# First experts of a four-block tower: up products by windows of 16 images, three of them without the class rows, and a ring for the split hidden rows

## The reference, cut to what matters

```python
h = conv tokens + position table                     # 25 patches an image
h = concat([broadcast(cls_tok), h], axis=1)          # the class token comes first
h = h + L0_attn(layernorm(h))                        # causal: token t sees tokens 0..t
x = layernorm(h)
g = softmax(x @ gate_w + gate_b)                     # 32 gates a token
for e in range(32):
    hid = gelu(x @ w1[e] + b1[e])                    # 192 -> 768
    h  += g[..., e] * (hid @ w2[e] + b2[e])          # 768 -> 192
```

## Time and profile before

| | us |
|---|---|
| median of 3 runs | 3105.53 (3105.32 to 3115.47) |
| the profiled execution | 3103.02, its span 3101.2 |
| TensorE busy | 2909.5, mean granted clock 0.961 |
| VectorE busy | 2093.5 |
| ScalarE busy | 1067.5 |
| GpSimd busy | 616.4 |

### The profile page before, as it was taken

One profiled execution on the slowest core, in us unless ns is written; L12 is line 12 of the kernel. 1 busy time (PEld: TensorE's weight loads), 2 busy tenths in 40 slices (PEclk: granted clock), 3 DMA queues, 4 the chain that ended last, 5 costly groups with the idle time before them and its releaser, 6 DMA issues. The chain is left out here.

```text
span 3101.2 us, 56587 instructions
## 1 busy us (share of the span) xinstructions
PE 2909.5 (94%) x20015; PEld 2670.3 (86%) x20015; DVE 2093.5 (68%) x5315; ACT 1067.5 (34%) x2124; POOL 616.4 (20%) x807
## 2 busy tenths in 40 slices
PE   9899999999999999999998998897998899958888
PEld 7779999999999999999997888675777889957677
DVE  3857677767767777777776776333448667777876
ACT  2533333323333333333233333112435433324433
POOL 1312111221212121111212100112213201122450
PEclk9989999999999999999999999798999989989999
DMA  3001100000100000000000000372000100000000
GB/s 136 26 30 36 37 18 36 36 36 18 36 36 19 35 36 36 18 36 36 18 31 9 2 2 2 94 240 73 1 11 1 54 19 19 1 11 16 23 19 17
DMA packets 24461, 105.56 MB, mean 34 GB/s; under 512 B 4455, under 2 KB 9463, under 8 KB 19086
## 3 DMA queue, kind: packets, MB, share of 16 engines
q1 hardware_dynamic: 22654, 99.62, 9.2%
q0 software_dynamic: 1584, 3.30, 0.3%
HBM read 98.32 MB, written 6.64 MB: 34 GB/s over the span
## 5 line engine op out<-in xcount | busy, mean ns | idle before, releaser
L907 ACT ACTIVATE hid<-bank,dat 128x384 f32<-128x384 f32 (+1 forms) x912 | 555.5, 610 | 1144.3 <-PE bank L597 1031.7
L872 PE MATMUL bank<-w,hid_hi 128*128 128x384 f32 x2964 | 859.3, 361 | 2.2 <-DVE y_tok L923 1.6
L874 PE MATMUL bank<-w,hid_lo 128*128 128x192 f32 x2964 | 745.8, 252 | 0.0
L874 PEld LDWEIGHTS bank<-w,hid_lo 128*128 128x128 f32 x2964 | 571.3, 193 | 1.7
L872 PEld LDWEIGHTS bank<-w,hid_hi 128*128 128x128 f32 x2964 | 561.7, 190 | 5.5 <-issue 3.9
L941 DVE TENSOR_TENSOR hid_lo<-hid,hid_hi 128x384 fp32r<-128x384 f32 (+1 forms) x912 | 540.0, 592 | 31.5
L938 DVE CAST hid_hi<-hid 128x384 fp32r<-128x384 f32 (+1 forms) x912 | 340.9, 374 | 126.4 <-ACT hid L907 125.3
L964 DVE SCALAR_TENSOR_TENSOR h_tok<-bank,gate,h_tok 128x192 f32<-128x192 f32 x416 | 173.5, 417 | 247.2 <-PE bank L874 243.8
L597 PE MATMUL bank<-xa_hi,w_hi 128*128 128x384 f32 (+1 forms) x912 | 324.6, 356 | 7.6 <-DVE w_lo L750 4.7
L597 PE MATMUL bank<-xa_lo,w_hi 128*128 128x384 f32 (+1 forms) x912 | 323.1, 354 | 0.0
L597 PE MATMUL bank<-xb,w_lo 128*128 128x384 f32 (+1 forms) x912 | 322.7, 354 | 0.0
(11 more groups left out here) (361 smaller groups left out, 4383.0 us busy)
## 6 DMA issues: line engine op xcount, KB each, us to landing
raw<-in_L_exp SPq DMA_DIRECT2D x36, 1344.0 KB, 5.6
w_e<-in_L_exp SPq DMA_DIRECT2D x20, 576.0 KB, 4.0
w_e<-in_L_exp SPq DMA_DIRECT2D x20, 384.0 KB
pix<-in_pixels SPq DMA_DIRECT2D x6, 832.0 KB, 10.2
w_e<-in_L_exp SPq DMA_DIRECT2D x20, 195.0 KB
raw<-in_L_mlp SPq DMA_DIRECT2D x2, 1344.0 KB, 5.7
wp_raw<-in_L_att SPq DMA_DIRECT2D x1, 2304.0 KB, 8.3
route_rows<-in_rows_clear SPq DMA_DIRECT2D x1, 2000.0 KB, 23.1
```

Of the source, the lines that this page charges most:

```text
L872: nc.tensor.matmul(o[:, 0:2 * D], hid_hi[k % 2][:, m, c], w2[j][:, m, :], start=m == 0, stop=False)
L874: ins = nc.tensor.matmul(o[:, 0:D], hid_lo[k % 2][:, m, c], w2[j][:, m, 0:D], start=False, stop=m == HC - 1)
L907: nc.scalar.activation(hid[(6 * k + m) % 3][:, 0:128 * nt], bank[4 + (6 * k + m) % 4][:, 0:128 * nt], func, bias=bias).then_inc(s["h_act"] ...
```

## The change

All experts now work by windows of 16 images, 416 columns, instead of 384 or 512. With `one_class=True`, which only the 32 first experts get, windows 1, 2 and 3 leave out the class column of each image in the up products and in the activation: the moving operand becomes a view of 25 slots by 16 images, image innermost, so that neighbouring columns lie 26 elements apart. The results stand side by side in the bank (400 columns), and ScalarE writes them back to their places in `hid`, with the same step. `hid` becomes six buffers of 416 columns, one for each m; its class columns are written in window 0 of each expert, and windows 1 to 3 leave them as they are. All 416 columns are still split, and the down products still run by the same 13 tiles.

`hid_hi` and `hid_lo` become one ring each of 896 columns (seven tiles). Since windows and tiles have different lengths, tile t is read at `RING_OF_TILE[t]`, and window 2 is written in two pieces, at the end and at the start of the ring.

```diff
+WINDOW = 16 * SLOT
+RING = 896
+RING_OF_WINDOW = [[(0, 416, 0)], [(0, 416, 416)], [(0, 64, 832), (64, 416, 0)], [(0, 416, 352)]]
+RING_OF_TILE = [0, 128, 256, 384, 512, 640, 768, 0, 128, 256, 384, 512, 640]
...
-        hid_hi = [sb("hid_hi0", [128, HC, 512], F32R, ex)]
+        hid = [sb(f"hid{j}", [128, WINDOW], scope=ex) for j in range(HC)]
...
-        hid = [sb(f"hid{j}", [128, 512], scope=ex) for j in range(3)]
-        hid_hi.append(sb("hid_hi1", [128, HC, 512], F32R, ex))
-        hid_lo = [sb(f"hid_lo{j}", [128, HC, 512], F32R, ex) for j in range(2)]
+        hid_hi = sb("hid_hi", [128, HC, RING], F32R, ex)
+        hid_lo = sb("hid_lo", [128, HC, RING], F32R, ex)
...
+            def patches(x, k):
+                return x.rearrange("p (m s) -> p s m", s=SLOT)[:, 1:, :] if one_class and k else x
+            def width(k):
+                return WINDOW - WINDOW // SLOT if one_class and k else WINDOW
+            def product_of(o, k):
+                o = o[:, 0:width(k)]
+                return o.rearrange("p (s m) -> p s m", m=WINDOW // SLOT) if one_class and k else o
...
                 def up(e, j, k):
-                    t0, nt = BLOCKS[k]
-                    c = slice(128 * t0, 128 * (t0 + nt))
+                    xh, xl, xbt = (patches(x[:, WINDOW * k:WINDOW * (k + 1)], k) for x in (xa_hi, xa_lo, xb))
...
-                        o = bank[4 + (6 * k + m) % 4][:, 0:128 * nt]
+                        o = product_of(bank[4 + (6 * k + m) % 4], k)
...
-                             xa_hi[:, c], xa_lo[:, c], xb[:, c], True).then_inc(s["h_full"].sem, 1)
+                             xh, xl, xbt, True).then_inc(s["h_full"].sem, 1)
...
                 def down(e, j, k):
-                        c = slice(128 * t, 128 * t + 128)
+                        c = slice(RING_OF_TILE[t0 + t], RING_OF_TILE[t0 + t] + 128)
...
-                            act.wait_ge(s["h_split"].sem, b["h_split"] + n - 2)
+                            act.wait_ge(s["h_split"].sem, b["h_split"] + n - 5)
...
-                            nc.scalar.activation(hid[(6 * k + m) % 3][:, 0:128 * nt],
-                                                 bank[4 + (6 * k + m) % 4][:, 0:128 * nt], func,
+                            nc.scalar.activation(patches(hid[m][:, :], k),
+                                                 product_of(bank[4 + (6 * k + m) % 4], k), func,
...
                 def split(e, j, k):
-                    prev = [TILES * e + BLOCKS[3][0], TILES * (e + 1), TILES * (e + 1) + BLOCKS[1][0],
+                    prev = [TILES * e + 11, TILES * (e + 1), TILES * (e + 1) + BLOCKS[1][0],
...
-                        nc.vector.tensor_copy(hid_hi[k % 2][:, m, 0:w], h).then_inc(s["dve_step"].sem, 1)
+                        for c0, c1, at in RING_OF_WINDOW[k]:
+                            ins = nc.vector.tensor_copy(hid_hi[:, m, at:at + c1 - c0], hid[m][:, c0:c1])
+                        ins.then_inc(s["dve_step"].sem, 1)
...
+                        for c0, c1, at in RING_OF_WINDOW[k]:
+                            ins = nc.vector.tensor_tensor(hid_lo[:, m, at:at + c1 - c0], hid[m][:, c0:c1],
+                                                          hid_hi[:, m, at:at + c1 - c0].bitcast(F32), ALU.subtract)
+                        ins.then_inc(s["h_split"].sem, 1)
...
-        experts_phase(32, a["L0_exp"], "L0_b1", "L0_b2", h_tok, ACT.Gelu, w, g, stats_of=h_tok)
+        experts_phase(32, a["L0_exp"], "L0_b1", "L0_b2", h_tok, ACT.Gelu, w, g, stats_of=h_tok, one_class=True)
```

More of the change, by code:

```diff
@@ L152, in vit_tower @@
         w2 = [sb(f"w2_{j}", [128, HC, 2 * D], F32R, ex) for j in range(2)]
-        hid_hi = [sb("hid_hi0", [128, HC, 512], F32R, ex)]
-        sb("ex_pad", [128, RAW_AT - 4 * 2 * HID - 4 * HC * D - HC * 512], scope=ex)
+        hid = [sb(f"hid{j}", [128, WINDOW], scope=ex) for j in range(HC)]
+        sb("ex_pad", [128, RAW_AT - 4 * 2 * HID - 4 * HC * D - HC * WINDOW], scope=ex)
         raw = [sb(f"raw{j}", [128, RAW], scope=ex) for j in range(2)]
-        hid = [sb(f"hid{j}", [128, 512], scope=ex) for j in range(3)]
-        hid_hi.append(sb("hid_hi1", [128, HC, 512], F32R, ex))
-        hid_lo = [sb(f"hid_lo{j}", [128, HC, 512], F32R, ex) for j in range(2)]
+        hid_hi = sb("hid_hi", [128, HC, RING], F32R, ex)
+        hid_lo = sb("hid_lo", [128, HC, RING], F32R, ex)
         ex.close()
@@ L774, in split_weights, with experts_phase @@
                                     ALU.subtract).then_inc(s["w_split"].sem, 1)
-        def experts_phase(E, dram, b1_col, b2_col, res, func, weights, gating=None, onto=None, stats_of=None):
+        def experts_phase(E, dram, b1_col, b2_col, res, func, weights, gating=None, onto=None, stats_of=None, one_class=False):
+            def patches(x, k):
[5 more added lines that the diff above has]
+                return o.rearrange("p (s m) -> p s m", m=WINDOW // SLOT) if one_class and k else o
             b = base(h_full=24 * E, h_act=24 * E, h_split=24 * E, y_full=TILES * (E + 1),
@@ L869, in down @@
                         o = bank[(t0 + t) % 4]
-                        c = slice(128 * t, 128 * t + 128)
+                        c = slice(RING_OF_TILE[t0 + t], RING_OF_TILE[t0 + t] + 128)
                         for m in range(HC):
-                            nc.tensor.matmul(o[:, 0:2 * D], hid_hi[k % 2][:, m, c], w2[j][:, m, :],
+                            nc.tensor.matmul(o[:, 0:2 * D], hid_hi[:, m, c], w2[j][:, m, :],
                                              start=m == 0, stop=False)
-                            ins = nc.tensor.matmul(o[:, 0:D], hid_lo[k % 2][:, m, c], w2[j][:, m, 0:D],
+                            ins = nc.tensor.matmul(o[:, 0:D], hid_lo[:, m, c], w2[j][:, m, 0:D],
                                                    start=False, stop=m == HC - 1)
@@ L898, in body @@
                 def body(e, j, i):
-                    for k, (t0, nt) in enumerate(BLOCKS):
+                    for k in range(4):
                         for m in range(HC):
@@ L926, in split @@
                 def split(e, j, k):
-                    t0, nt = BLOCKS[k]
-                    w = 128 * nt
-                    prev = [TILES * e + BLOCKS[3][0], TILES * (e + 1), TILES * (e + 1) + BLOCKS[1][0],
+                    prev = [TILES * e + 11, TILES * (e + 1), TILES * (e + 1) + BLOCKS[1][0],
                             TILES * (e + 1) + BLOCKS[2][0]][k]
@@ L936, in split @@
                         dve.wait_ge(s["h_act"].sem, b["h_act"] + n + 1)
-                        h = hid[(6 * k + m) % 3][:, 0:w]
-                        nc.vector.tensor_copy(hid_hi[k % 2][:, m, 0:w], h).then_inc(s["dve_step"].sem, 1)
+                        for c0, c1, at in RING_OF_WINDOW[k]:
+                            ins = nc.vector.tensor_copy(hid_hi[:, m, at:at + c1 - c0], hid[m][:, c0:c1])
+                        ins.then_inc(s["dve_step"].sem, 1)
                         dve.wait_ge(s["dve_step"].sem, b["dve_step"] + STEPS * e + 6 * k + m + 1
                                     + (BLOCKS[k - 1][0] if k > 1 else 0))
-                        nc.vector.tensor_tensor(hid_lo[k % 2][:, m, 0:w], h,
-                                                hid_hi[k % 2][:, m, 0:w].bitcast(F32),
-                                                ALU.subtract).then_inc(s["h_split"].sem, 1)
+                        for c0, c1, at in RING_OF_WINDOW[k]:
+                            ins = nc.vector.tensor_tensor(hid_lo[:, m, at:at + c1 - c0], hid[m][:, c0:c1],
+                                                          hid_hi[:, m, at:at + c1 - c0].bitcast(F32), ALU.subtract)
+                        ins.then_inc(s["h_split"].sem, 1)
                 def total(t):
```

## The result

| | before | after |
|---|---|---|
| median, us (4 runs each, beside each other) | 3107.99 (3105.32 to 3115.47) | 3702.37 (3695.08 to 3709.15) |
| ratio | | 1.192 (1.189 to 1.195) |
| the profiled execution, us | 3103.02 | 3704.34 (span 3702.6) |
| stage of the 32 first experts, us | 1452.3 | 2041.5 |
| all the rest of the profiled execution, us | 1650.7 | 1662.8 |

19% slower: 594 us, where the forecast had 415 (3520 us; range 3078 to 3640). The direction and the mechanism were forecast, the size was not, and the time lies above the range. 589 of the 601 us between the two profiled executions are in the stage of the first experts (from its first up product to the first product behind it).

The account below looks back on a forecast made before the run. TensorE's matmul stream was taken to bound the 32 first experts. 3103.0 - 20.8 (fewer columns) + 435 (stepped columns) = 3517 us; the median being 2.5 us higher, 3520 us. Forecast 3430 to 3640, 8-in-10 range 3078 to 3640.

Parts of the forecast that it names:

- What bounds the stage: In the 32 first experts only TensorE's stream of matmuls sets the time: busy 1300 of 1300 us at clock 1.00.
- Fewer columns, -20.8 us: Up products of the 32 first experts: 1616 columns instead of 1664 at 0.451 ns each, 20.8 us less in sum.
- The price of the stepped column: Up windows 1 to 3: 0.833 ns a stepped column, 0.151 us more a matmul, 435 us more over 2880.
- rival B: Up windows 1 to 3: TensorE held to VectorE's 1.37 ns a stepped column, 4138 us in all; chance 0.06.
- rival A: Up windows 1 to 3: stepped reads are free, only the column count matters, 3085 us in all; chance 0.33.
- Down products, 0: Down products of the experts keep number and size, 1.70 us a tile: no change in time.
- ScalarE: Stepped activation writes, 18 of an expert's 24, take up to 0.88 us, hidden by up products at 0.91 us: no cost.
- VectorE's split in two pieces: Window 2, where the ring wraps: 0.30 us more a unit, 1.8 us an expert, hidden; at most 58 us if uncovered.
- GpSimd: Splitting the next expert's weights after the last split: 3.3 us of room before TensorE needs them, and the room stays.
- The other six experts, 0: Experts outside the 32 first go to four windows of 416, the same 1664 columns: no change.
- D: Up windows 1 to 3: mild step cost of 0.05 to 0.2 ns a column, 3140 to 3320 us; chance 0.06.
- C: Window 2: stepped reads free, but VectorE's 1.8 us of splits reach TensorE through the banks, whole 3142 us; chance 0.03.

Follow-up runs that it names:

- the two halves of the change: Two runs of the changed kernel: only the moving operand read side by side, 3098.56 us; only ScalarE's write side by side, 3699.2 us.
- the plain windows: The changed kernel without leaving out the class columns, four windows of 416 adjacent columns, ring and two-piece splits kept: 3116.29 us, ratio 1.002.
- run 2: Not a run: these characters occur only in "run 2% slower", said of the down products behind some stepped up products.

## Why the prediction was right in kind and wrong in size

- *What bounds the stage*, right: TensorE was busy all of it in both kernels, and 589 of the 601 us between the profiled executions came out of its stream. No other engine's change reached it in the kernel after.
- *Fewer columns, -20.8 us*, right: window 0 ran on the line at 0.189 us a matmul, and 400 contiguous columns took 182.7 ns where 182.4 was worked out. With the copied columns 15 to 16 us of the 20.8 showed in the stage. The formula by column count that the prediction takes from the Trainium skill (TensorE: Matmul & The Clock Gate, Back-to-back issue gap) is given there for an isolated matmul and not for a stream; by it 400 columns would take 169 ns, an estimate from the page, which neither 182.7 nor 386 agrees with.
- *The price of the stepped column*, the step that failed. The text took "one column in every second clock of TensorE", 0.833 ns. Stepping was forecast to cost 0.151 us a matmul and cost 0.204 (0.213 in window 2). The two clocks are nearly what some steps cost: steps of 8 to 48 that are multiples of eight have 0.845 to 0.856. But the change's own step is 26, and it costs 0.966: 0.386 us a matmul, not 0.333, 0.053 x 2880 = 153 us; window 2 adds 9 ns x 960 = 9 us. The upper side of the range was bounded by "the doubled column", 0.902, so that the range ended at 3640; the measured value lay between that and rival B's 1.37. The lower of the two values between which the price was chosen, 0.77, came from VectorE's row at a step of 5 elements. Its rows at 20 and 26 elements, the change's own distance, had 0.6 to 0.7 ns more, so 1.05 to 1.15 in sum; they stood in the text and were used neither for the value nor as an end of the range. They are too high for TensorE as well, whose surplus is 0.515 ns. That the direction was right owes something to luck: only rows of another engine carried it against rival A's 0.33.
- *Down products, 0*, wrong by a small term: a pair of high and low takes 0.2896 us behind the stepped windows and 0.2838 with contiguous ones (144.8 and 141.9 ns a matmul), 0.49 us an expert, 16 us. They return to 142 with the ring kept and the read contiguous, so it is not the ring. The slowing goes with the window directly in front: views with steps of 16, of 26, 28 and 64 in rows of 16, and pairs at a step of 26, give 144.6 to 145.3 ns; steps of 2 to 8, 20, 24, 27, 32, 40, 48, 26 in rows of 50 or 64, and 64 in rows of 26 in most experts, give 141.9 to 142.4. Why is not explained.
- *ScalarE*, wrong number (1.05 us where at most 0.88 was said; the step costs 457/400 = 1.14 ns an element, not up to 0.7), right conclusion: hidden, as the two halves of the change showed. The argument for it, that 0.88 is less than the 0.91 us of an up chunk, did not hold; it is hidden in the kernel after because a chunk takes 1.93 us there.
- *VectorE's split in two pieces*, right: 0.31 us a unit for 0.30, and never waited for in the kernel after. Its share was forecast at 75% to 77% (its own rows give 77% to 78%) and came out at 54%, since the stage is longer. The 1.75 us at the turn of the loop were not in the text; they cost nothing in the kernel after.
- *GpSimd*, right: its last step for the next expert ends at 1084.6, 3.4 us before the 1088.0 at which TensorE begins it (room of 3.3 was read).
- *The other six experts, 0*: the stage of four experts and what follows take 340 us instead of 337 in all kernels with the ring: some 3 us that were not forecast. About 1.3 us of them lie in the four experts (193.3 us before, 194.2 to 194.7 with the ring), the rest behind them; no run shows why.
- *The rivals.* A (columns are all that counts, chance 0.33) has its effect when the operand is contiguous and is excluded for the kernel as it is. B's 1.37 ns and D's surplus of 0.05 to 0.2 ns are excluded by 0.966, C by the plain windows.

The sum with measured terms: 3103.0 - 20.8 + 435 + 153 + 9 + 16 + 3 = 3698 us, against 3704.3 in the profiled execution. Within the stage the terms make 592 us where 589 were measured. Outside it 3 of 12 us are named, and the rest is of the size of what the last attention stage took more: 187.6 us after, 177.3 before. That stage differs as much between executions of one and the same kernel, 187.4 and 178.2 us with the copied columns, with a granted clock of 0.78 to 0.95 in its stretches of 30 us in the one and 0.83 to 1.00 in the other; so it is not put down to the change.

## What to carry to other kernels

A matmul of this type (fp32r) that is fed through a view is not priced by its column count alone: whole aligned groups of four columns ran at full speed here, and where there were none a matmul took 1.9 to 2.4 times as long a column. Leaving out one column in 26 by a stepped view cost 600 us (3699.2 less 3098.56) for the 20.8 that it was to save. With the kept columns copied side by side once (1.2 us a buffer) and used 32 times, 15 to 16 us of the gain came back. When no row shows the engine in question doing the new thing, let the range reach to the dearest row of another engine at the same step.

## What the runs showed of the hardware that was not expected

- A moving operand of type fp32r: full speed for aligned runs of four columns (16 bytes), half for pairs and for a step of 2; steps of 8 to 48 that are multiples of eight columns 0.845 to 0.856 ns a column, 26 at 0.966 to 1.04, 64 at 1.03 to 1.09. The granted clock was 1.00 there, but with a step of 64 in rows of 26 it fell to 0.50 for 3.4 us in most of that step's windows, with TensorE busy and no slower for it.
- ScalarE writing 400 elements: 594 ns side by side, 596 in runs of 25, 1051 with a step of 104 bytes.
- The down products, whose operands did not change, run 2% slower (144.6 to 145.3 ns a matmul for 141.9) behind some stepped up products.
- Behind the turn of the loop VectorE stood idle for 1.7 to 2.0 us ahead of its second instruction, in the kernel after, with the plain windows and with the copied columns, and not in the kernel before; as long as TensorE is slow it costs nothing.
